# Other step lists for the first and the middle batches of a gated cross-attention and expert kernel, on all engines

## The chip, the cores and the metric

The kernel runs on one core of a Trainium2 chip. The metric is the device time of one execution in microseconds. TensorE is called PE, VectorE DVE, ScalarE ACT, GpSimd POOL and SyncE SP, as the profile does.

## The reference, cut to what matters

x is 8 batches x 512 tokens x 256, the context 8 x 512 x 128. There are 16 heads of 64 and 8 experts of which each token takes 2.

```python
x = x + tanh(g_xattn) * (softmax(q k^T / 8) v @ Wo + bo)   # q = layernorm(x) @ Wq, k, v = ctx @ Wk, ctx @ Wv
h = layernorm(x)
comb = top2(softmax(h @ gate_w.T))                          # 8 weights per token, 6 of them zero
x = x + tanh(g_ffn) * sum_e comb[:, e] * (h @ expert_w[e].T + expert_b[e])
```

## The kernel before

Each fp32 operand is split into two fp16 parts, high and low, and each product is made of three fp16 matmuls (high x high, high x low, low x high).

A batch is worked through in 32 rows, one for each pair of heads p and each tile t of 128 queries (32 = 8 pairs x 4 tiles). The attention of unit n of a batch goes through all engines: PE makes its scores (`scores`, line 1480, six matmuls for the two heads) into one of two PSUM buffers ST, used in turn; DVE takes the negative row maximum (`maximum`, line 1021) and adds a constant (`shift`, line 1027); ACT makes the exponential pf (`exp`, line 832), which frees ST, and copies it to fp16 (`copy`, line 842, p_s high); POOL subtracts to get the low part (`low`, line 654); SP transposes both halves by DMA into pt_s (lines 554 and 561); PE multiplies them with the values (`values`, line 1502, 24 matmuls) and DVE divides (`normalise`, lines 1041 and 1044). pf has 3 slots, p_s 4 and pt_s 8, so that `exp` of unit n waits for `low` of n - 3, `copy` and `low` of n for the transposes of n - 4, and the transpose of n for `values` of n - 8.

Between the scores PE does jobs, each into one of three shared PSUM banks MB in turn: q, k, v (projections, 6, 3 and 3 matmuls), xt and x2t (transposed normalised inputs), ot (transposed outputs of a pair of heads), wo (output projection, 12 matmuls), logits, gates, bias, bound and pair (two tiles through one expert, 12 matmuls). A job of the kind q, k, v, xt, ot or x2t is taken out by ACT (`hi`, high part) and then by DVE (`take`, low part); the others by DVE alone. A job needs the bank of the third job before it, so the `take` of that one.

In what order each engine does all this is written out by hand, one string for each row, in `PE_ORDER`, `ACT_ORDER`, `DVE_ORDER` and `POOL_ORDER`, each with one list for the first batch (`FIRST`), one for the six middle batches (`LOOP`) and one for the last (`LAST`). Every engine walks its own list and waits for semaphores. The n-th `take` or `hi` of a list means the n-th job of PE's list, so a new PE list renumbers them. `values` runs 6 units behind: the first six `values` of a list belong to the batch before (in the first batch they are skipped), and `VALUES_BACK` and its like set that. SP has no list: it walks units in order, `turn_hi` and `turn_lo` of each (lines 554 and 561), with the store of the batch before (line 593) and the load of the next context (line 570) ahead of unit 0, and the load of the next x (line 583) behind unit 9.

In the first batch DVE and ACT also split Wo and the expert weights (`ll`, line 1213, and `lh`, line 817), after maxima (`lm`) and scales (`ls`, with PE's `lsum`). `context` on ACT splits the next context and waits for c_mul, which DVE makes when it takes the job `bound`. `sums1` and `moments1` on DVE (lines 877 and 886) and `power1` and `norm1` on POOL normalise the next x; the same with 2 is for the experts. `route1` to `route3` on DVE choose the experts, and `hold1` to `hold3` make POOL stand still meanwhile.

## Time and profile before

| what | us |
|---|---|
| median of 3 runs (lowest, highest) | 945.15 (944.91, 945.45) |
| the profiled execution, its own time | 948.67 |
| its span, first to last instruction | 946.9 |
| PE, DVE, ACT, POOL busy | 902.7, 852.6, 743.8, 646.3 |

The profiled execution lies 3.5 us above the median, and its span 1.8 us below its own time. The stages are told by the maxima of unit 0 of each batch: the first batch goes from 22.8 to 133.9 us, each middle batch takes 109.7 us (the sixth 111.4 in this execution), and the last goes from 793.7 to the end. A row of a timeline is a time of start, a duration, engine, line and tiles, and in square brackets the idle time of that engine before it and what ended it.

### The profile page before, as it was taken

Reading aid. Unit: us, or ns where it says so; the run is one execution under the profiler, and the core shown is the slowest. Engines: PE = TensorE matmul, PEld = TensorE weight load, DVE = VectorE, ACT = ScalarE, POOL = GpSimd, SP = SyncE. Lnnn points to the kernel's source line nnn. Section 1 sums busy time; section 2 is a strip of 40 time slices with the busy share of each in tenths; the row PEclk is TensorE's granted clock in tenths of the full one; section 3 lists DMA queues with packets and bytes.
Section 4 is the critical chain, followed back from the end, with each engine's and each line's share of the span. In section 5 each row is a group of like instructions: output and inputs, shape, how many; then the busy total and the mean of one; then the engine's idle time right before and its main releaser. Section 6 shows DMA issues by size and latency. Waiting matters only on the chain.

```text
span 946.9 us, 28867 instructions
## 1 busy us (share of the span) xinstructions
PE 902.7 (95%) x11376; PEld 605.1 (64%) x11376; DVE 852.6 (90%) x1853; ACT 743.8 (79%) x1093; POOL 646.3 (68%) x449
## 2 busy tenths in 40 slices
PE   6788799999999999999999999999999999999997
PEld 4245455777657776677657776577655776667873
DVE  6899799998999989999899989999899998999768
ACT  3898899778995879958896879958899588988510
POOL 4677768677695867768586776958687686877400
PEclk9899899999999999999999999999999999999999
DMA  6699899999999999989999999989999799999900
GB/s 222 143 179 167 146 161 190 165 150 165 171 193 149 158 148 197 183 141 157 180 180 160 153 162 189 186 146 157 150 187 187 137 154 171 169 169 164 143 24 23
DMA packets 549142, 150.97 MB, mean 159 GB/s; under 512 B 537592, under 2 KB 547216, under 8 KB 548752
## 3 DMA queue, kind: packets, MB, share of 16 engines
q1 hardware_dynamic: 549008, 149.13, 94.7%
q8 instruction: 91, 1.49, 0.6%
q14 instruction: 43, 0.35, 0.1%
HBM read 11.70 MB, written 4.19 MB: 17 GB/s over the span
## 4 chain that ended last, share of the span: by engine, by line
PE 47%; DVE 25%; ACT 12%; issue 8%; DMA 3%; POOL 3%; SPq 1%; ACTq 0%; DVEq 0%; POOLq 0%
PE MB L1338 24%; PE ST L1480 9%; PE PV L1502 9%; DVE nmax L1021 8%; ACT pf L832 5%; ACT p_s L842 4%; PE MB L1350 3%; DMA pt_s<-p_s 3%; POOL p_s L654 2%; DVE acc L956 2%; DVE QL L1001 2%; DVE x L924 1%; DVE o_n L1044 1%; DVE v_s L1012 1%; ACT v_s L758 1%
## 5 line engine op out<-in xcount | busy, mean ns | idle before, releaser
L654 POOL TENSOR_TENSOR p_s<-pf,p_s 128x1024 f16<-128x1024 f32 x254 | 542.1, 2136 | 217.3 <-ACT p_s L842 169.1
L832 ACT ACTIVATE pf<-ST,shifts 128x512 f32<-128x512 f32 x512 | 324.4, 691 | 92.2 <-DVE shifts L1027 89.9
L1021 DVE TENSOR_REDUCE nmax<-ST 128x2 f32<-128x1024 f32 x256 | 310.4, 1217 | 17.6 <-PE ST L1480 15.8
L842 ACT ACTIVATE p_s<-pf 128x1024 f16<-128x1024 f32 x254 | 270.7, 1069 | 3.2
L1502 PEld LDWEIGHTS PV<-v_s,pt_s 128*128 128x128 f16 x6096 | 204.3, 98 | 43.6 <-issue 27.5
L1502 PE MATMUL PV<-v_s,pt_s 128*128 128x65 f16 x6096 | 215.7, 193 | 4.7 <-DVE o_n L1044 2.7
L1338 PE MATMUL MB<-ex_s,x2t_s 128*128 128x256 f16 (+1 forms) x1380 | 166.8, 276 | 1.1 <-DVE x L924 1.0
L1338 PEld LDWEIGHTS MB<-ex_s,x2t_s 128*128 128x128 f16 x1380 | 131.7, 98 | 23.6 <-DVE x L924 2.3
L1480 PE MATMUL ST<-KH,QH 64*128 64x512 f16 x512 | 100.8, 390 | 16.3 <-ACT pf L832 14.0
L975 DVE SCALAR_TENSOR_TENSOR acc<-MB,m,acc 128x256 f32<-128x256 f32 x224 | 95.6, 476 | 4.4 <-PE MB L1338 3.6
L1480 PE MATMUL ST<-KH,QL 64*128 64x512 f16 x512 | 99.0, 383 | 0.0
L1480 PE MATMUL ST<-KL,QH 64*128 64x512 f16 x512 | 98.8, 382 | 0.0
L1338 PE MATMUL MB<-xt_s,wq_s 128*128 128x512 f16 x384 | 95.0, 384 | 2.8 <-DVE ot_s L1009 1.3
L1338 PE MATMUL MB<-wo_s,ot_s 128*128 128x256 f16 x744 | 91.8, 274 | 0.1
L1338 PEld LDWEIGHTS MB<-wo_s,ot_s 128*128 128x128 f16 x744 | 71.5, 98 | 17.2 <-DVE v_s L1012 2.6
L1480 PEld LDWEIGHTS ST<-KH,QH 64*128 64x128 f16 x512 | 24.9, 93 | 77.8 <-ACT pf L832 34.4
L1338 PEld LDWEIGHTS MB<-xt_s,wq_s 128*128 128x128 f16 x384 | 33.1, 98 | 45.2 <-issue 12.9
L1001 DVE SCALAR_TENSOR_TENSOR QL<-MB,q_out,QH 128x512 f16<-128x512 f32 x64 | 47.5, 743 | 12.4 <-ACT QH L743 12.4
L1044 DVE TENSOR_TENSOR o_n<-PV,rden 128x256 f32<-128x256 f32 x127 | 53.9, 425 | 4.4
L1338 PE MATMUL MB<-wv_s,kv_s 128*128 128x512 f16 x192 | 53.9, 394 | 2.5 <-DVE QL L1001 1.9
L1012 DVE SCALAR_TENSOR_TENSOR v_s<-MB,v_mul,v_s 128x512 f16<-128x512 f32 x64 | 47.0, 748 | 7.8 <-ACT v_s L758 6.4
L1338 PE MATMUL MB<-kv_s,wk_s 128*128 128x512 f16 x192 | 52.3, 382 | 1.4 <-DVE KL L1001 1.3
(174 smaller groups left out, 986.5 us busy)
## 6 DMA issues: line engine op xcount, KB each, us to landing
pt_s<-p_s SPq DMA_TRANSPOSE x508, 3.4
xin<-x SPq DMA_DIRECT2D x7, 512.0 KB, 4.9
out<-acc SPq DMA_DIRECT2D x7, 512.0 KB, 3.9
kvin<-kv_t SPq DMA_DIRECT2D x8, 256.0 KB, 4.4
stage_e<-expert_t SPq DMA_DIRECT2D x1, 2048.0 KB, 11.1
stage_o<-wo SPq DMA_DIRECT2D x1, 1024.0 KB, 5.8
stage_q<-wq SPq DMA_DIRECT2D x1, 768.0 KB, 7.3
xin<-x SPq DMA_DIRECT2D x2, 256.0 KB, 2.9
```

The lines of the kernel that those rows point to most:

```text
L654: pool.tensor_tensor(p_s[:, slot, 1, :, :], pf[:, it.ring(p, u, PF_SLOTS), :, :], p_s[:, slot, 0, :, :], ALU.subtract).then_inc(p_lo, 1)
L832: last = act.activation(pf[:, (n - 1) % PF_SLOTS, i, :], ST[u % 2][:, i, :], ACT.Exp, bias=shifts[:, u % 2, i:i + 1])
L842: act.activation(p_s[:, it.ring(p, u, P_SLOTS), 0, :, :], pf[:, it.ring(p, u, PF_SLOTS), :, :], ACT.Copy).then_inc(p_hi, 1)
L975: last = dve.scalar_tensor_tensor(acc[:, t, :], m[:, DIM * i:DIM * (i + 1)], comb[:, t, e:e + 1], acc[:, t, :], ALU.mult, ALU.add)
L1001: last = dve.scalar_tensor_tensor(l_s[:, slot_, :], m[:, :], scale, h_s[:, slot_, :], ALU.mult, ALU.subtract)
L1012: last = dve.scalar_tensor_tensor(v_s[:, 1, t, g * HH:(g + 1) * HH, 0:HEAD], m[:, :].rearrange("p (h d) -> p h d", d=HEAD), v_mul[:, it.b ...
L1021: dve.tensor_reduce(nmax[:, t % 2, :, 0], ST[t % 2][:, :, :], AX.X, ALU.max, negate=True)\
L1044: dve.tensor_tensor(dst, outs[:, :, 0:HEAD], rden[:, :].unsqueeze(2).broadcast_to([P, TT, HEAD]), ALU.mult).then_inc(o_ready, 1)
L1338: last = pe.matmul(dst, s, m, start=(k == 0), stop=(k == n - 1))
L1350: last = pe.transpose(bank_[:, tile(t)], src(t), ident[:, :])
L1480: last = pe.matmul(ST[t % 2][:, i, :], queries[r, s, tile(t)], keys[r, s, :], start=(n == 0), stop=(n == len(terms) - 1))
L1502: last = pe.matmul(dst, pt_s[:, slot, a, i, k, :], v_s[:, c, k, (2 * p + i) % HEADS, :], start=(k == 0 and n == 0), stop=(k == TT - 1 and ...
```

## The change

The lists of `FIRST` and `LOOP` are replaced for all four engines; those of `LAST` stay, and so does every other line. Each list holds the same steps as often as before (in `LOOP` 129 for PE, 102 for ACT, 153 for DVE, 42 for POOL; in `FIRST` 105, 111, 144 and 37), in another order, and PE's jobs are taken out in that new order. The core of the diff; of DVE's list for the first batch only the new rows are shown. Rows are counted from 0 within a list:

```diff
@@ -68,25 +68,25 @@
 
 PE_ORDER = {
     FIRST: (
-        "scores", "scores pj q2", "scores v0,0 v3,0 values", "scores v1,0 values", "scores",
-        "scores values values v2,0 k2", "scores values q3", "scores q4", "scores values values values",
-        "scores v0,1 values", "scores k3 k4 values", "scores k5", "scores q5", "scores values values lsum ot0 v1,1",
-        "scores", "scores values values v3,1", "scores values values", "scores q6 ot1 values values", "scores v2,1",
-        "scores values k7 values k6", "scores values values", "scores wo0,0 values bound", "scores wo0,1 values ot3",
-        "scores q7 ot2", "scores values values", "scores xt1 values xt0 wo1,1", "scores values", "scores wo1,0 k1",
-        "scores values values q0", "scores values ot4 ot5 values", "scores k0", "scores q1 wo2,0 wo2,1",
+        "scores", "scores pj", "scores v1,0 values values values v3,0", "scores v2,0 v0,0 values",
+        "scores values q2 values", "scores k2 k3 values", "scores values q3", "scores", "scores v0,1", "scores v1,1 k4",
+        "scores values values q4", "scores values values ot0 v2,1", "scores values lsum", "scores v3,1 values", "scores",
+        "scores values values values bound values", "scores k5", "scores values values q5 ot1", "scores q6",
+        "scores wo0,0 values", "scores wo0,1", "scores k6 k7", "scores values q7", "scores ot3 values",
+        "scores ot2 values xt1", "scores values values xt0", "scores values values",
+        "scores wo1,1 values values wo1,0 ot4", "scores", "scores values ot5 q0 k0", "scores values k1",
+        "scores q1 wo2,0 wo2,1",
     ),
     LOOP: (
-        "scores", "scores v3,0 values v2,0 values", "scores", "scores ot6 values values q2 values values",
-        "scores ot7 k2", "scores v0,0 wo3,1", "scores v1,0 wo3,0 v1,1", "scores values q3 values", "scores",
-        "scores q4 values values k3", "scores v3,1 v0,1", "scores k5 values values x2t0 ot0",
-        "scores x2t1 q5 bound values values", "scores ot1 v2,1 logits values values k4", "scores",
-        "scores q6 wo0,0 values values pair0,3 pair0,6 values wo0,1", "scores",
-        "scores values pair1,1 pair1,7 pair0,5 pair0,1 pair1,0", "scores", "scores values ot2 pair1,5 values q7",
-        "scores", "scores values ot3 gates values pair0,0 k6 bias1", "scores", "scores k7 values values pair0,2 wo1,0",
-        "scores", "scores xt0 wo1,1 pair1,4 pair0,4 xt1", "scores",
-        "scores values ot4 values pair1,3 pair0,7 values values", "scores", "scores bias0 q1 k1 values q0 pair1,6 ot5",
-        "scores", "scores values k0 wo2,0 pair1,2 wo2,1",
+        "scores", "scores v1,0 values v2,0 values", "scores v3,0 values values", "scores v0,0 values ot6",
+        "scores k2 values q2", "scores ot7 values values", "scores k3 values", "scores v0,1 wo3,1",
+        "scores wo3,0 values q3", "scores", "scores k4 values ot0 values q4", "scores values bound q5 k5 values",
+        "scores v1,1 x2t1 x2t0", "scores values ot1 values logits v2,1", "scores wo0,1 wo0,0 v3,1 values", "scores",
+        "scores values q6 values k6 pair0,0 pair1,6 values pair0,3", "scores",
+        "scores pair1,4 pair1,7 pair0,1 values pair1,0", "scores", "scores pair1,3 q7 values pair0,6 ot2", "scores",
+        "scores pair1,1 values values pair1,2", "scores", "scores ot3 pair0,7 gates k7 values values pair0,5", "scores",
+        "scores pair0,4 xt0 values wo1,0 bias1 values bias0 xt1", "scores", "scores values wo1,1 values",
+        "scores ot4 q0 ot5 values pair1,5 k0 values", "scores", "scores k1 wo2,1 q1 pair0,2 wo2,0",
     ),
     LAST: (
...
@@ -103,18 +103,18 @@
 
 ACT_ORDER = {
     FIRST: (
-        "exp", "exp ph copy hi hi hi copy", "exp hi copy", "exp copy", "exp hi copy", "exp hi copy", "exp hi copy",
-        "exp hi copy", "exp hi copy", "exp hi copy", "exp hi copy", "exp hi copy", "exp hi copy", "exp lh copy lh",
-        "exp lh copy hi", "exp lh hi copy hi", "exp hi copy", "exp hi lh copy", "exp lh hi copy", "exp hi copy hi",
-        "exp context copy lh", "exp lh hi copy", "exp hi hi copy", "exp lh copy lg", "exp hi copy", "exp hi lh copy",
-        "exp lh copy", "exp lh hi copy hi", "exp hi copy hi", "exp hi copy", "exp hi copy", "exp copy",
+        "exp", "exp ph copy hi hi hi copy", "exp hi copy", "exp hi copy", "exp hi copy", "exp hi copy", "exp hi copy",
+        "exp hi copy", "exp hi copy hi", "exp copy", "exp hi copy hi", "exp hi copy", "exp hi copy lh",
+        "exp lh copy lh lh", "exp lh copy", "exp lh lh hi lh copy", "exp hi copy", "exp hi copy", "exp hi copy lh",
+        "exp lg copy", "exp hi copy hi", "exp hi copy", "exp hi copy", "exp hi copy", "exp hi copy", "exp lh copy hi",
+        "exp context copy lh", "exp hi lh copy", "exp hi hi copy hi", "exp hi copy", "exp hi copy", "exp copy",
     ),
     LOOP: (
-        "exp", "exp copy hi hi hi copy", "exp hi copy", "exp hi copy hi", "exp hi copy", "exp hi copy", "exp copy",
-        "exp copy hi hi", "exp hi copy", "exp hi hi hi copy hi", "exp hi hi hi copy hi", "exp copy", "exp hi copy hi",
-        "exp hi copy logits hi", "exp", "exp copy copy", "exp copy", "exp copy", "exp hi copy", "exp copy hi hi",
-        "exp copy", "exp hi copy hi", "exp copy", "exp copy hi", "exp context copy", "exp copy hi hi", "exp copy",
-        "exp copy", "exp hi copy hi hi", "exp hi copy hi", "exp copy", "exp copy",
+        "hi exp hi copy", "exp hi copy", "exp hi copy hi", "exp hi copy", "exp hi hi copy", "exp hi copy", "exp hi copy",
+        "exp copy", "exp copy hi hi hi", "exp hi copy", "exp hi hi copy", "exp hi hi hi copy hi", "exp hi copy logits",
+        "exp copy", "exp hi copy hi hi", "exp copy", "exp copy", "exp copy", "exp copy", "exp hi copy", "exp hi copy",
+        "exp copy", "exp copy hi", "exp hi copy", "exp copy context hi", "exp copy", "exp copy hi", "exp copy",
+        "exp hi hi hi copy", "exp copy hi hi", "exp hi copy", "exp copy",
     ),
     LAST: (
...
@@ -127,32 +127,31 @@
 
 DVE_ORDER = {
     FIRST: (
...
+        "maximum shift rq", "maximum shift pt", "maximum take shift", "maximum take shift take", "maximum lm shift take",
+        "maximum take shift lm", "maximum normalise take shift lm", "maximum take shift lm",
+        "maximum normalise take shift bound", "maximum normalise normalise shift take",
+        "maximum take take normalise shift lm", "maximum normalise shift lm", "maximum take shift",
+        "maximum ls normalise shift sums1", "maximum",
+        "maximum shift take shift moments1 normalise ll take take take normalise", "maximum",
+        "maximum shift take ll shift ll ll", "maximum take shift take normalise", "maximum ll shift take",
+        "maximum take shift ll", "maximum take shift", "maximum take shift take normalise", "maximum ll shift take",
+        "maximum normalise take shift", "maximum take normalise shift ll take", "maximum normalise shift gp",
+        "maximum take shift take ll normalise take", "maximum take shift ll ll", "maximum take shift",
+        "maximum take take shift take", "maximum ll shift normalise take take take",
     ),
     LOOP: (
-        "maximum shift", "maximum shift normalise", "maximum take shift take normalise",
-        "maximum shift take normalise take", "maximum take shift", "maximum take take shift take",
-        "maximum take shift take", "maximum shift sums2 moments2 normalise", "maximum shift take take",
-        "maximum shift bound take", "maximum take shift normalise take take",
-        "maximum take shift take take normalise take", "maximum shift take normalise take",
-        "maximum shift take take take normalise", "maximum",
-        "maximum shift take take shift take route1 normalise route2 route3 take take", "maximum",
-        "maximum shift shift take take take sums1 take normalise moments1 take", "maximum shift",
-        "maximum take shift take normalise take", "maximum shift take", "maximum take shift take take normalise",
-        "maximum take shift take", "maximum shift normalise take take take", "maximum shift",
-        "maximum take shift take take take", "maximum shift take normalise take", "maximum shift take take normalise",
-        "maximum shift take take", "maximum take shift take take", "maximum take shift",
-        "maximum take take shift normalise take take",
+        "maximum shift", "maximum shift normalise take", "maximum take shift normalise take", "maximum take shift bound",
+        "maximum shift take normalise", "maximum take shift normalise take take", "maximum shift take",
+        "maximum shift take", "maximum take shift take sums2 normalise moments2", "maximum take shift",
+        "maximum normalise take take take shift", "maximum shift take take take",
+        "maximum normalise take take take shift", "maximum shift take take normalise take",
+        "maximum take shift sums1 take", "maximum take normalise route1 take shift",
+        "maximum take route2 shift route3 take take", "maximum take shift normalise take",
+        "maximum shift take moments1 take take", "maximum shift", "maximum take shift take take normalise",
+        "maximum shift", "maximum shift take take normalise take", "maximum take shift take",
+        "maximum shift take take normalise take", "maximum", "maximum take shift shift take take take take normalise",
+        "maximum shift take", "maximum take normalise shift", "maximum take take take shift take normalise",
+        "maximum shift take take take", "maximum take shift take take",
     ),
     LAST: (
...
@@ -171,14 +170,14 @@
 
 POOL_ORDER = {
     FIRST: (
-        "residual low", "low", "low", "low", "low", "low", "low", "low", "low", "low", "low", "low", "low", "low", "low",
-        "low", "power1 low", "low", "low", "low", "low", "norm1 low", "low", "low", "low", "context low", "low",
-        "scale low", "low", "low", "low", "low",
+        "low", "residual low", "low", "low", "low", "low", "low", "low", "low", "low", "low", "low", "low", "low", "low",
+        "power1 low", "norm1 low", "low", "low", "low", "scale low", "low", "low", "low", "low", "low", "low", "low",
+        "context low", "low", "low", "low",
     ),
     LOOP: (
-        "low", "low", "low", "low", "low", "low", "low", "low", "low", "power2 low", "norm2 low", "residual low", "low",
-        "low", "low", "hold1 hold3 hold2 low", "low", "low", "low", "power1 low", "low", "norm1 low", "low", "low", "low",
-        "scale low", "context low", "low", "low", "low", "low", "low",
+        "low", "low", "low", "low", "low", "low", "low", "low", "low", "low", "power2 norm2 low", "residual low", "low",
+        "low", "low", "hold1 low", "hold2 hold3 low", "low", "low", "power1 low", "low", "low", "low", "low", "norm1 low",
+        "low", "low", "low", "scale context low", "low", "low", "low",
     ),
     LAST: (
```

## Rows read from the trace of the kernel before

**Rows 1.** The page: busy us of PE (share of the span), instructions.

```profile
PE 902.7 (95%) x11376; PEld 605.1 (64%) x11376; DVE 852.6 (90%) x1853; ACT 743.8 (79%) x1093; POOL 646.3 (68%) x449
```

**Rows 2.** Windows: length, busy us (instructions) by engine, PE clock, DMA share, GB/s.

```profile
22.80:133.90 111.10, 91.72 (x1035) 48.63 (x1031) 101.21 (x182) 96.23 (x145) 78.54 (x47) 0.91 0.94 161
...
243.55:353.24 109.69, 108.68 (x1420) 74.21 (x1418) 101.47 (x225) 91.36 (x135) 80.60 (x55) 1.00 1.03 166
...
682.31:793.67 111.36, 108.84 (x1420) 74.46 (x1418) 102.08 (x225) 91.36 (x135) 80.58 (x55) 1.00 1.00 165
```

**Rows 3.** Timeline of PE in the second middle batch.

```profile
242.69 0.39 PE L1480 MATMUL ST<-KH,QH 64*128 64x512 f16 x2
...
244.74 0.89 PE L1502 MATMUL PV<-v_s,pt_s 128*128 128x65 f16 x24
245.47 0.81 PE L1338 MATMUL MB<-wv_s,kv_s 128*128 128x512 f16 x3
...
246.93 0.39 PE L1480 MATMUL ST<-KH,QH 64*128 64x512 f16 x2
...
265.31 0.39 PE L1480 MATMUL ST<-KH,QH 64*128 64x512 f16 x2
...
265.96 0.38 PE L1480 MATMUL ST<-KH,QH 64*128 64x512 f16 x2
...
266.71 1.47 PE L1338 MATMUL MB<-xt_s,wq_s 128*128 128x512 f16 x6
268.01 1.62 PE L1502 MATMUL PV<-v_s,pt_s 128*128 128x65 f16 x48
...
281.50 0.39 PE L1480 MATMUL ST<-KH,QH 64*128 64x512 f16 x2 [0.50 <-ACT pf L832]
...
282.25 0.66 PE L1350 MATMUL MB<-ident,o_n 128*128 128x128 f32 x4
282.75 0.81 PE L1338 MATMUL MB<-wv_s,kv_s 128*128 128x512 f16 x3
...
301.66 4.10 PE L1338 MATMUL MB<-ex_s,x2t_s 128*128 128x256 f16 x36 [0.25 <-DVE x L924]
305.69 0.39 PE L1480 MATMUL ST<-KH,QH 64*128 64x512 f16 x2
```

**Rows 4.** Waits in that batch: us in total, times, longest us.

```profile
PEld ST L1480 <- ACT pf L832: 3.1, 8, 0.6
```

**Rows 5.** Timeline of SP in the second and the third middle batch.

```profile
252.28 1.33 SPq L561 DMA_TRANSPOSE pt_s<-p_s  x1
...
258.68 1.34 SPq L561 DMA_TRANSPOSE pt_s<-p_s  x1
...
278.25 1.31 SPq L561 DMA_TRANSPOSE pt_s<-p_s  x1
...
367.54 1.32 SPq L561 DMA_TRANSPOSE pt_s<-p_s  x1
```

**Rows 6.** The tile pt_s: from issue to landing of its transposes, us.

```profile
DMA to landing us min/median/max: 3.0/3.4/6.1
```

**Rows 7.** Waits in the first batch.

```profile
DVE nmax L1021 <- PE ST L1480: 8.0, 6, 3.4
```

**Rows 8.** Timelines of ACT and of DVE in the first batch.

```profile
96.17 0.72 ACT L789 ACTIVATE kv_s<-kvin,c_mul 128x512 f16<-128x512 f32 x1 [3.62 <-DVE c_mul L985]
...
67.89 0.14 DVE L1168 TENSOR_SCALAR eb_mul<-late_mul 128x1 f32<-128x1 f32 x1
...
101.09 1.23 DVE L1021 TENSOR_REDUCE nmax<-ST 128x2 f32<-128x1024 f32 x1 [3.39 <-PE ST L1480]
```

**Rows 9.** Timeline of SP in the first batch, and the tile xin: issue to landing.

```profile
64.61 0.53 SPq L583 DMA_DIRECT2D xin<-x  x1
...
DMA to landing us min/median/max: 2.8/4.5/5.5
```

**Rows 10.** The tile ex_s: ns of one min/median/max, first and last start.

```profile
L1213 DVE SCALAR_TENSOR_TENSOR ex_s<-stage_e,late_mul,ex_s x8: 741/923/1716, 93.0 to 131.1; 128x512 f16<-128x512 f32 x8
```

11 lines of the change are left out of this document (removed).

## The prediction

> **What bounds the kernel now.** The page's busy line comes first: PE is busy 95% of the span, DVE 90% [rows 1]. That is an average over three stages, so I cut the span at the maxima of unit 0 of each batch and read the windows [rows 2]. In a middle batch PE is busy 108.68 of 109.69 us at full clock, DVE 101.47 and ACT 91.36: PE bounds it, six times. In the first batch PE has 91.72 of 111.10, DVE 101.21 and ACT 96.23: DVE bounds it, with 9.9 us of idle. The last batch keeps its lists. So two sums are wanted: PE's waits and its fixed work in the middle, DVE's waits in the first. PE's timeline gives the price of each step [rows 3], the waits who holds it up [rows 4], SP's timeline and the landing of pt_s when the transposes come [rows 5, 6]; for the first batch the same of DVE and ACT [rows 7 to 10].
>
> The profiled execution takes 3.5 us more than the median of the runs. 1.67 of it is the sixth middle batch (111.36 for 109.69), the rest lies outside what changes; the difference is added to the median.
>
> **Middle batches, PE's fixed work.** No step is added or removed; what the order alone changes is how often PE goes from scores to a job and back. Start to start, scores behind scores take 0.65 (265.31 to 265.96), scores before a job 0.75 (265.96 to 266.71), q 1.30 (266.71 to 268.01), values 0.73 (244.74 to 245.47), ot 0.50 (282.25 to 282.75). v and values behind it, up to the scores, take 1.46 (245.47 to 246.93), so v 0.65 and about 0.1 for the way back; three pairs 4.03 (301.66 to 305.69), so 1.31 each and again 0.1 [rows 3]. So a row that holds jobs costs 0.2 more than one of scores alone. Old list: 12 rows are scores alone, 20 hold jobs. New list: 10 and 22. That is +0.4 per batch. With 32 scores, 32 values, 8 q, 16 k and v and the rest at these prices the old list adds up to 107.4 without a wait, the new to 107.8. The other 2.3 of the 109.69 are waits: ACT's exponentials have up to 3.1 in total by the view of waits, 0.6 the longest [rows 4] (part of it overlaps the running matmuls), as the 0.50 at 281.50, where ACT comes out of rows 9 to 12 with eight copies of projections behind it; and takes of DVE, as the 0.25 at 301.66 [rows 3].
>
> **Middle batches, the waits of ACT and DVE.** The new lists put the steps of ACT and of DVE nearer to PE's own order. The eight `hi` that the old list of ACT has in its rows 9 and 10 are ten in rows 8 to 11 in the new one (3, 1, 2, 4), behind copies of units that PE needs no sooner. Walking both engines along PE's new rows at the durations of before I find slack of 0.1 to 0.7 us where the old lists had none. I take 0.5 for all that is left (0 to 2.3: none, or as much as before). DVE's `bound` goes from row 9 to row 3 and there needs the load of the context, behind the store at SP's head; DVE isn't the bound and has 8 us of slack in the batch. Cost 0, up to 1 where PE waits for the take behind it.
>
> **Middle batches, the transposes.** This is what speaks against the change. SP issues them back to back, 1.3 us each (1.33, 1.34, 1.31, 1.32) [rows 5], so two to a unit, 64 to a batch, 85 us; the first ten or so units queue behind one another, since exponentials run ahead of them. The new list takes `values` closer behind: units 0 and 1 in row 5 (7 before), unit 2 in row 6 (9), unit 9 in row 13, units 11 to 13 in row 16 (15, 15, 17). Whether PE then stands is a race that can be counted. Unit 2: ahead of its `values` in the new list stand 7 scores (4.55), 4 v (2.6), 8 values (5.84), 2 k (1.3), 1 q (1.3), 2 ot (1.0) and 5 ways there and back (1.0), together 17.6 us behind the first scores. Its low transpose was issued 16.0 behind them (258.68 - 242.69 [rows 3, 5]) and in the next batch 15.2 (367.54 - 352.38, that is 242.69 and a batch); its landing takes 3.4 in the median [rows 6], so it is there at 19.4 or 18.6; less 0.5, by which the exponentials of the first units come earlier in my walk of the new lists, since the old ones end a batch with ACT behind PE. PE waits 0.5 to 1.3, the mean is 0.9. Unit 9, counted in the same way (14 scores, 15 values, 6 v, 4 k, 4 q, 4 ot, two of wo at the price of a pair, two x2t at that of ot, the small `bound`, 12 rows there and back): 39.5 us of work, the transpose issued at 35.6 (278.25 - 242.69) and landed at 39.0, or at 41.7 with the longest landing of 6.1. PE waits 0 to 2.2; I take 0.5, nearer to what the median landing gives. Units 11 to 13 have a few tenths of margin. What PE loses in the front it doesn't lose again behind, since the transposes catch up. Sum of the transposes: 1.4; the lower bound is nothing (0.5 for unit 2 is within the error of my walk), the upper 1.3 + 2.2 = 3.5.
>
> So a middle batch takes 107.8 + 0.5 + 1.4 = 109.7, as before: +0.0 each, with bounds of -1.4 (0.5 for everything) and +1.6 (3.5 instead of 1.4, less the 0.5 of other waits, which it covers).
>
> The Trainium skill ("DMA: Bandwidth & Descriptors", section "Latency and other measured facts") gives 261 GB/s for DMA transposes; for our 256 KB each that is an estimate of 1.0 us, where the trace has 1.3 [rows 5]. By the page the queue of the first ten units would be 0.3 x 2 us shorter per unit, 1.8 us at unit 2, and the waits above would be gone; that is the rival "to the floor" below, with 108.3 per batch. The trace decides, so I don't take it.
>
> **The first batch.** DVE's idle there is led by 8.0 us of maxima that wait for scores, 3.4 the longest [rows 7]; 1.56 of the 8.0 lies ahead of the window. The longest comes so: `bound` stands in row 21 of PE and row 22 of DVE, `context` in row 20 of ACT. ACT stands 3.62 us for c_mul at 96.17, the exponentials behind it are late, ST isn't free, and DVE stands 3.39 at 101.09 [rows 8]. In the new lists the job stands in row 15 of PE and its take in row 15 of DVE, `context` in row 26 of ACT: it finds c_mul made. -3.4. Its rows move behind the stall, and nobody waits for them but the first projections of the next batch, seven rows on. Of the other 3.1 us of that kind about half goes, since ACT's `lh` and `hi` are spread more evenly and DVE's maxima of rows 14 and 16 stand alone: -1.5 (0 to -3.1). Against it `sums1` moves from row 15 to row 13. It needs the load of x that SP issues at 64.61, landing 4.5 later in the median, at 69.1, at the latest at 70.1 [rows 9]; DVE ends `ls` at 68.0 (67.89 + 0.14 [rows 8]) and would have a division and a shift (0.7, an estimate) to do before `sums1`: it waits 0.4 to 2.1 (from none of it done to the latest landing), more if it keeps a better pace until then. I take 1.5, because I let some of the early waits go. A further 0.2 for `bound` and `moments1` standing nearer to their givers. Sum: -3.4 - 1.5 + 1.5 + 0.2 = -3.2 (-5 to -1).
>
> What the splits `ll` take isn't sure: the eight of ex_s took 741 to 1716 ns, the median 923 [rows 10]. All at the lowest would give back 8 x 0.18 = 1.5 us, and as much could come on top. I take 0, because POOL has a `low` in every row of either list. With that the bounds of the first batch are -5 and 0.
>
> The Trainium skill ("SBUF — State Buffer", section "Who interferes with whom") says that a DVE instruction with two SBUF inputs and a GpSimd instruction that reads SBUF shut one another out for their whole length, which speaks for the long ones [rows 10]. By the page the spread depends on which of the two is issued first; if all eight met a `low` and took the 1716 of the longest, the sum would be 8 x 0.79 = 6.3 us more, and I see nothing in the new order that makes more of them meet.
>
> **Total.** 945.15 - 3.2 + 6 x 0.0 = 942.0 (rounded).
>
> **The rivals.**
> - To the floor. The transposes are early enough, because ACT and POOL start each batch sooner and shorten the whole queue: 107.8 + 0.5 = 108.3, 6 x -1.4, with the first batch 945.15 - 8.4 - 3.2 = 933.6. For it: the store and the load at SP's head don't depend on the lists, and 0.9 us of wait is small beside a landing of 3.0 to 6.1 [rows 6]. Against it: SP is full from unit 0 to unit 9 whatever ACT does [rows 5].
> - The transposes bind (the other side). With the longer landings units 2 and 9 cost 3.5 together, 111.3 a batch: 945.15 + 9.6 - 3.2 = 951.6. It decides from 1.9 us of transpose waits a batch on, where 945.15 is reached. For it: a landing can take 6.1 [rows 6], and the sixth middle batch lost 1.67 in this execution [rows 2]. Against it: the five others lost none.
> - The change doesn't do in the first batch what it seems to: the stall of `context` is only moved. The wait for x at its upper bound, splits beside POOL +1: 0 instead of -3.2, 945.2. For it: DVE has 101.2 of fixed work, and where ACT (96.2) no longer stands, DVE's own order does [rows 2].
>
> **How the numbers follow.** Forecast 0.36, to the floor 0.19, transposes bind 0.23, no gain in the first batch 0.22. A measurement of this kernel tells 0.2%, 1.9 us, from no change: faster is below 943.3, slower above 947.0. The forecast's own range is 939 to 945: 0.26 of its 0.36 is faster, 0.10 same. The floor is faster, the binding case slower. The fourth is 0.05 faster, 0.14 same, 0.03 slower. Faster 0.50, same 0.24, slower 0.26. The range goes from the floor's 933.5 to 951.0, just short of the binding case's bound, and leaves out a tenth at either end.
>
> **What the profile of the changed kernel would show.** Middle batches between the maxima of unit 0: near 109.7; 108.3 would be the floor. Waits of values for pt_s about 1.4 a batch, near rows 6 and 13, where there were almost none; waits of scores for exponentials about 0.5 instead of 3.1. First batch near 107.9, with no wait of `context` for c_mul, one of `sums1` for x of 0.4 to 2.1. The prediction is wrong if the transposes are issued otherwise than back to back, if PE's clock falls below full in a middle batch, or if DVE's queue meets a job's take that I took to be covered.

## The result, and the profile after

The changed kernel takes 954.87 us in the median of six runs (950.31 to 958.13), the kernel before 945.03 in six runs beside it (943.66 to 947.99). The ratio is 1.0101, with a 95% interval of 1.0076 to 1.0125: 1% slower, where 942.0 was forecast, and outside the range of 933.5 to 951.0. The runs spread wider than those of before, over 7.8 us instead of 4.3. The profiled execution is the fastest of the six (950.31, span 948.5), so what it shows is a mild case.

The page after, first row, answers to [rows 1]; busy times have hardly moved, which is right for lists of the same steps.

```profile
PE 899.2 (95%) x11376; PEld 606.0 (64%) x11376; DVE 854.0 (90%) x1853; ACT 751.2 (79%) x1093; POOL 646.0 (68%) x449
```

The windows by batch answer to [rows 2], with the same columns: the first batch and the first four middle ones.

```profile
21.69:129.61 107.92, 88.55 (x1037) 47.84 (x1034) 101.86 (x181) 96.52 (x145) 78.14 (x47) 0.96 0.98 169
129.61:238.27 108.66, 107.78 (x1414) 74.20 (x1413) 101.60 (x226) 91.87 (x134) 80.27 (x54) 1.00 1.02 164
238.27:349.13 110.86, 108.59 (x1420) 74.73 (x1418) 101.69 (x225) 92.72 (x135) 80.70 (x55) 1.00 1.01 165
349.13:463.17 114.04, 110.02 (x1420) 75.13 (x1418) 101.79 (x225) 92.75 (x135) 80.69 (x55) 0.99 1.01 161
463.17:574.07 110.90, 108.80 (x1420) 74.71 (x1418) 101.78 (x224) 92.60 (x135) 80.67 (x55) 1.00 1.03 165
```

The middle batches, of which five took 109.7 before and the sixth 111.4, now take anything from 108.7 to 114.0. (The window of the first holds six matmuls fewer than the others, 1414 instead of 1420, so its 108.66 flatters it.) All six together are 666.0 (129.61 to 795.60) for 659.8 before. The first batch is 107.9, as forecast, in this execution.

What lengthens the third middle batch is seen on PE's timeline, ahead of the values of unit 2 (its first scores start at 348.27), and on SP's, where the low transpose of that unit is the row of 363.59.

```profile
365.95 0.82 PE L1337 MATMUL MB<-kv_s,wk_s 128*128 128x512 f16 x3
368.71 1.34 PE L1501 MATMUL PV<-v_s,pt_s 128*128 128x65 f16 x24 [1.95 <-issue]
369.99 0.61 PE L1479 MATMUL ST<-KH,QH 64*128 64x512 f16 x2
```

```profile
354.36 0.48 SPq L569 DMA_DIRECT2D kvin<-kv_t  x1
354.93 1.89 SPq L553 DMA_TRANSPOSE pt_s<-p_s  x1
356.88 2.54 SPq L560 DMA_TRANSPOSE pt_s<-p_s  x1
359.50 1.26 SPq L553 DMA_TRANSPOSE pt_s<-p_s  x1
360.82 1.33 SPq L560 DMA_TRANSPOSE pt_s<-p_s  x1
362.24 1.30 SPq L553 DMA_TRANSPOSE pt_s<-p_s  x1
363.59 1.33 SPq L560 DMA_TRANSPOSE pt_s<-p_s  x1
```

The transpose is issued 15.3 us behind the first scores and lands 5.0 later, where the median is 3.4 [rows 6]; the values start then, after 1.95 of idle. "issue" says that the profile names no releaser for that row; in sister batches the same row is ended by the DMA of pt_s. SP has no gap. Two transposes of unit 0 took 1.89 and 2.54 instead of 1.3; in the third middle batch of the kernel before the same two took 1.9 and 2.4, so that alone is nothing new. The wait costs more than its length: the values behind it take 1.34 for 0.89 [rows 3], the scores 0.61 for 0.39, for the granted clock is half in that stretch. Two windows show it. It is the only middle batch of this profile where the clock fell; the fourth had a wait of 1.76 ahead of the same values and kept it.

```profile
366.00:369.00 3.00, 1.05 (x14) 0.47 (x13) 2.96 (x6) 2.76 (x5) 2.28 (x2) 0.99 1.24 123
369.00:372.00 3.00, 3.00 (x28) 1.45 (x26) 0.76 (x2) 0.89 (x2) 1.65 (x1) 0.50 0.98 184
```

The same batch has the other place, row 16, ahead of the values of unit 11.

```profile
401.96 0.88 PE L1501 MATMUL PV<-v_s,pt_s 128*128 128x65 f16 x24 [1.36 <-DMA pt_s<-p_s]
```

The kernel before had that wait too, once: the 1.7 us that its sixth middle batch took longer are nearly all a wait for the transpose of unit 11, in its row 15.

```profile
731.42 0.88 PE L1502 MATMUL PV<-v_s,pt_s 128*128 128x65 f16 x24 [1.50 <-DMA pt_s<-p_s]
```

### The profile page after: what moved, and what is told of

Its sections match the earlier page's. It is cut to its first block, busy times and chain, and to the rows that moved or that the text cites. A ratio compares the mean times of both kernels' runs of the same rounds, so it can differ in the third digit from the quotient of the medians.

```text
span 948.5 us, 28867 instructions
## 1 busy us (share of the span) xinstructions
PE 899.2 (95%) x11376; PEld 606.0 (64%) x11376; DVE 854.0 (90%) x1853; ACT 751.2 (79%) x1093; POOL 646.0 (68%) x449
## 4 chain that ended last, share of the span: by engine, by line
PE 58%; DVE 16%; issue 7%; ACT 7%; DMA 6%; POOL 5%; SPq 1%; ACTq 0%; DVEq 0%; POOLq 0%
PE MB L1337 29%; PE ST L1479 12%; PE PV L1501 11%; POOL p_s L653 4%; DVE nmax L1020 4%; ACT pf L831 4%; DMA pt_s<-p_s 3%; PE MB L1349 3%; ACT p_s L841 3%; DMA kvin<-kv_t 1%; PE ST L1337 1%; DVE QL L1000 1%; DVE acc L955 1%; DVE o_n L1043 1%; DVE ot_s L1008 1%
## 5 line engine op out<-in xcount | busy, mean ns | idle before, releaser
L1501 PEld LDWEIGHTS PV<-v_s,pt_s 128*128 128x128 f16 x6096 | 210.2, 98 | 58.7 <-issue 36.5
L1501 PE MATMUL PV<-v_s,pt_s 128*128 128x65 f16 x6096 | 222.2, 194 | 14.8 <-DMA pt_s<-p_s 7.4
L1337 PE MATMUL MB<-ex_s,x2t_s 128*128 128x256 f16 (+1 forms) x1380 | 170.3, 276 | 0.2
L1337 PEld LDWEIGHTS MB<-ex_s,x2t_s 128*128 128x128 f16 x1380 | 129.7, 98 | 32.6 <-DVE acc L974 7.3
L1479 PEld LDWEIGHTS ST<-KH,QH 64*128 64x128 f16 x512 | 25.4, 93 | 68.0 <-issue 27.1
L742 ACT ACTIVATE QH<-MB,q_out 128x512 f16<-128x512 f32 x64 | 44.8, 700 | 21.2 <-PE MB L1337 20.7
L746 ACT ACTIVATE KH<-MB,k_mul 128x512 f16<-128x512 f32 x64 | 45.2, 706 | 17.1 <-PE MB L1337 16.9
L1337 PEld LDWEIGHTS MB<-xt_s,wq_s 128*128 128x128 f16 x384 | 35.1, 99 | 34.4 <-issue 2.9
L757 ACT ACTIVATE v_s<-MB,v_mul 128x512 f16<-128x512 f32 x64 | 45.0, 708 | 11.2 <-PE MB L1337 11.2
```

Source lines behind the costliest of these rows:

```text
L742: last = act.activation(QH[:, it.pair_slot(name), :], m[:, :], ACT.Copy, scale=q_out[:, of % 2:of % 2 + 1])
L746: last = act.activation(KH[:, it.pair_slot(name), :], m[:, :], ACT.Copy, scale=k_mul[:, of % 2:of % 2 + 1])
L757: last = act.activation(v_s[:, 0, t, g * HH:(g + 1) * HH, 0:HEAD], m[:, :].rearrange("p (h d) -> p h d", d=HEAD), ACT.Copy, scale=v_mul[:, ...
L1337: last = pe.matmul(dst, s, m, start=(k == 0), stop=(k == n - 1))
L1479: last = pe.matmul(ST[t % 2][:, i, :], queries[r, s, tile(t)], keys[r, s, :], start=(n == 0), stop=(n == len(terms) - 1))
L1501: last = pe.matmul(dst, pt_s[:, slot, a, i, k, :], v_s[:, c, k, (2 * p + i) % HEADS, :], start=(k == 0 and n == 0), stop=(k == TT - 1 and ...
```

## The experiments

A number such as 945.5 beside them is the median of the kernel before in the same set of runs, on the same chip. Where experiments of different sets are set against one another, the sets' own medians of the kernel before lie between 945.2 and 945.8.

**New lists for the first batch only.**

```diff
 FIRST: new on all four engines
 LOOP:  old on all four engines
```

> New lists for the first batch on all engines, the old ones for the middle batches. In the changed kernel's profile unit 0 of the second batch starts 4.3 us earlier than before (129.6 against 133.9). Theory (the first batch gains, the middle batches lose by late transposes): 945.0 - 4.3 = 940.7, middle batches 109.7 each as before. Rival (the first batch's gain is of that one execution, or is given back at the seam of the lists): 945.

Measured: 950.79 (944.11 to 952.43, 10 runs) for 945.48, ratio 1.0045 (1.0026 to 1.0064). Both guesses fell: the kernel does not gain 4.3, it loses 5.3. Four of its six middle batches are 109.7 to 109.8 as before, the two others 110.8 and 111.3; the first batch is 115.13 in this profile. One of the ten executions took 944.11, so the list can also run as fast as the old one.

```profile
21.26:136.39 115.13, 92.86 (x1037) 50.40 (x1034) 104.50 (x182) 96.90 (x145) 78.49 (x47) 0.90 0.89 159
```

The same list took 107.92 in the changed kernel's profile, so two executions of one list can be laid side by side. They part in rows 13 to 20. First DVE in this experiment:

```profile
68.27 1.41 DVE L878 BATCH_NORM_STATS2 stats<-xin 128x6 f32<-128x256 f32 x4 [2.04 <-DMA xin<-x]
...
82.00 2.38 DVE L1214 SCALAR_TENSOR_TENSOR wo_s<-stage_o,late_mul,wo_s 128x512 f16<-128x512 f32 x1
84.31 0.14 DVE L1028 TENSOR_REDUCE shifts<-nmax 128x2 f32<-128x4 f32 x1
84.38 3.27 DVE L1214 SCALAR_TENSOR_TENSOR wo_s<-stage_o,late_mul,wo_s 128x512 f16<-128x512 f32 x2
```

and the same in the changed kernel:

```profile
67.62 1.41 DVE L876 BATCH_NORM_STATS2 stats<-xin 128x6 f32<-128x256 f32 x4 [0.95 <-DMA xin<-x]
...
79.51 1.95 DVE L1212 SCALAR_TENSOR_TENSOR wo_s<-stage_o,late_mul,wo_s 128x512 f16<-128x512 f32 x1
81.39 0.14 DVE L1026 TENSOR_REDUCE shifts<-nmax 128x2 f32<-128x4 f32 x1
81.45 1.40 DVE L1212 SCALAR_TENSOR_TENSOR wo_s<-stage_o,late_mul,wo_s 128x512 f16<-128x512 f32 x2
```

Then PE in this experiment:

```profile
73.62 1.48 PE L1503 MATMUL PV<-v_s,pt_s 128*128 128x65 f16 x24 [2.75 <-DVE o_n L1045]
...
90.16 2.74 PE L1339 MATMUL MB<-wo_s,ot_s 128*128 128x256 f16 x12 [3.49 <-DVE ot_s L1010]
```

and in the changed kernel:

```profile
72.98 0.88 PE L1501 MATMUL PV<-v_s,pt_s 128*128 128x65 f16 x24 [1.20 <-DVE o_n L1043]
...
85.36 1.49 PE L1337 MATMUL MB<-wo_s,ot_s 128*128 128x256 f16 x12 [0.62 <-DVE ot_s L1008]
```

DVE waits a us more for x, and the division comes 0.65 later (73.05 for 72.40). PE is 0.9 ahead here and stands 2.75 for it instead of 1.20. The clock had fallen to half ahead of that wait in both (68.7 here, 68.5 there, behind 2.0 us of idle for the exponentials); there it is full again from 72.0, here only from 79.0, and the 24 matmuls take 1.48 for 0.88. In row 17 the three splits beside POOL start 2.5 later and take 5.65 for 3.35, the take of ot1 is 4.8 late, PE stands 3.49 instead of 0.62, and the clock is at half again until 96.0. Between the two executions lie 7.2 us.

DVE's own work has grown as well. Its busy time in the first batch is 104.5 here, 104.3 to 104.6 in four more profiles of the new list and 101.9 in the changed kernel's, but 99.1 to 102.2 in seven profiles of the old one. The splits are a part of it (15.7 us for the twelve here, 14.3 in the profile before). The other part is one instruction of the step `gp`, moved from row 30 to row 26, which the prediction doesn't mention: the split of the expert bias, 0.47 us in every profile of the old list and 2.40 to 2.43 in all six of the new. The tile view before and here:

```profile
L1175 DVE SCALAR_TENSOR_TENSOR eb_s<-eb,eb_mul,eb_s x1: 474/474/474, 128.6 to 128.6; 8x256 fp32r<-8x256 f32 x1
L1176 DVE SCALAR_TENSOR_TENSOR eb_s<-eb,eb_mul,eb_s x1: 2414/2414/2414, 115.3 to 115.3; 8x256 fp32r<-8x256 f32 x1
```

**New lists for the middle batches only.**

```diff
 FIRST: old on all four engines
 LOOP:  new on all four engines
```

> Old lists for the first batch, new ones for the middle batches. Theory: the loss is all in the middle, 954.9 + 4.3 = 959.2, some 2.3 us for each of the six batches. Rival (the loss needs both, since the new first list hands the middle batches a worse start): 945 to 950.

Measured: 952.25 (950.84 to 957.54, 5 runs), ratio 1.0087 (1.0060 to 1.0113). The middle lists lose 6.8 us by themselves, 1.1 a batch. With the 5.3 of the first lists that is 12.1 for the 9.8 measured together: within the spread of the runs, the two losses add up. The theory had put all of it in the middle and was half right.

**Six values moved back.**

```diff
 PE:  -"scores ot7 values values", "scores k3 values", "scores v0,1 wo3,1"
      +"scores ot7", "scores k3 values values", "scores v0,1 wo3,1 values"
      -"scores values q6 values k6 pair0,0 pair1,6 values pair0,3"
      +"scores q6 k6 values pair0,0 values pair1,6 pair0,3 values"
 DVE: division of units 0, 1 from row 5 to row 6, of 10, 11 from row 15 to row 16
```

> The changed kernel, with only the values of units 0 to 2 (one row later, behind the jobs of their row) and of units 11 to 13 (behind q6 and k6 in the same row) moved back in the middle list of PE, and the two divisions behind them on DVE. Theory (PE stands only for transposes that have not landed, since SP issues them back to back): those waits go, a middle batch takes about 108.1, 954.9 - 6 x 3.9 = 931.5; at least below 940. Rival (the new order of the takes and the exponentials is what makes PE wait, late transposes only stand in its place): 950 to 957, with waits of scores and jobs for ACT and DVE in their place.

Measured: 960.99 (958.74 to 966.74, 4 runs), ratio 1.0175 (1.0140 to 1.0210). A miss, and its own fault. Units 0 to 2 no longer wait in its profile, but the values of unit 12 need the division of units 10 and 11, which the edit had put behind the take of k6, and PE stands there for 1.75 to 1.90 us in each of the six middle batches. In three of them it comes back slow (here 14 matmuls of the pairs in 2.69 us, where the 12 ahead of the wait took 1.47):

```profile
297.52 1.47 PE L1380 MATMUL MB<-ex_s,x2t_s 128*128 128x256 f16 x12
300.89 0.89 PE L1544 MATMUL PV<-v_s,pt_s 128*128 128x65 f16 x24 [1.90 <-DVE o_n L1086]
301.62 2.69 PE L1380 MATMUL MB<-ex_s,x2t_s 128*128 128x256 f16 x14
```

That gives the price of a fall of the clock, since the wait is nearly the same everywhere: with the fall a batch takes 112.2, 112.7 and 113.1, without it 111.0 to 111.3, so some 1.5 us more. The third and the sixth batch, both with 1.90 us of wait there:

```profile
359.71:472.76 113.05, 110.12 (x1420) 75.72 (x1418) 101.79 (x225) 92.58 (x135) 80.66 (x55) 0.98 0.99 162
694.83:806.12 111.29, 108.44 (x1420) 74.86 (x1418) 101.84 (x225) 92.61 (x135) 80.69 (x55) 1.00 1.00 165
```

So the length of that wait alone doesn't tell which it will be. The front and row 16 were parted, below.

**SP's store and load later.**

```diff
 SP, middle batches:
-store, load of the next context, unit 0, unit 1, unit 2, ...
+unit 0, unit 1, unit 2, store, load of the next context, unit 3, ...
 DVE: bound from row 3 to row 9
```

> The changed kernel, with the store and the load of the next context behind the transposes of unit 2 instead of ahead of those of unit 0 in SP's order of the middle batches, and bound in row 9 of DVE instead of row 3, since its load comes later. Theory: the transposes of units 0 to 2 are issued about 1.2 us sooner (0.58 + 0.48 and the gaps), the wait for unit 2 shrinks by that, those for units 11 to 13 stay: 954.9 - 6 x 1.1 = 948. Rival (not SP's queue but the copies and low parts set when the transposes go, or the takes of DVE set PE's waits): no change, 955.

Measured: 952.21 (948.00 to 953.49, 5 runs), ratio 1.0066 (1.0044 to 1.0087), 2.7 below the changed kernel (the two intervals overlap, so the gain in time is likely, not certain). In its second middle batch (first scores at 244.51) the low transpose of unit 2 is issued 14.0 behind them, and its values follow k3 without a wait; nowhere in the fronts of its six middle batches is there one of 0.3 us or more:

```profile
258.55 1.33 SPq L580 DMA_TRANSPOSE pt_s<-p_s  x1
259.93 0.58 SPq L616 DMA_DIRECT2D out<-acc  x1
260.62 0.48 SPq L589 DMA_DIRECT2D kvin<-kv_t  x1
```

```profile
261.53 0.82 PE L1361 MATMUL MB<-kv_s,wk_s 128*128 128x512 f16 x3
262.19 0.90 PE L1525 MATMUL PV<-v_s,pt_s 128*128 128x65 f16 x24
```

No list of PE, ACT or POOL differs from the changed kernel's, and on DVE only `bound` stands elsewhere, so it is SP's queue that the front waits for. (That `bound` had a share wasn't tested by itself, but the waits that went had been for the transposes.) Of the expected 6.6 us only 2.7 came. The waits in row 16 stay, as expected; new ones, for the transposes of units 5 and 6, stand in rows 10 and 11 in four of the six batches, 0.92 to 1.66 us:

```profile
385.86 0.88 PE L1525 MATMUL PV<-v_s,pt_s 128*128 128x65 f16 x24 [1.66 <-DMA pt_s<-p_s]
```

**Front values later**, with the old first list.

```diff
 PE:  -"scores ot7 values values", "scores k3 values", "scores v0,1 wo3,1"
      +"scores ot7", "scores k3 values values", "scores v0,1 wo3,1 values"
 DVE: -"maximum take shift normalise take take", "maximum shift take"
      +"maximum take shift take take", "maximum shift take normalise"
```

> Old first list, new middle lists, and in these only the values of units 0 to 2 one row later (with the division of units 0 and 1). Baseline is the kernel with the old first and the new middle lists, 952.3. Theory (in the front PE stands for transposes that are late by 0.8 to 2.2 us a batch, and most of it is given back once it stands less, some of it is taken again at row 16, where PE now comes earlier): 946, between 943 and 949. Rival (as the kernel with six values moved back, which took 961: moving values costs PE more than it saves): 952 or more.

Measured: 946.17 (943.25 to 948.49, 10 runs) for 945.34, ratio 1.0014 (1.0003 to 1.0025). The theory's number: 6.1 us of the 6.8 come back by three `values` moved by one row, with the division of two units.

**Front and row 16 later.**

```diff
 as above, and
 PE:  -"scores values q6 values k6 pair0,0 pair1,6 values pair0,3"
      +"scores q6 values k6 pair0,0 values pair1,6 pair0,3 values"
 DVE: -"maximum take normalise route1 take shift"
      +"maximum take route1 take shift normalise"
```

> As the one before, and in row 16 the values of unit 11 behind q6 and those of unit 12 behind pair0,0, with the division of units 10 and 11 at the end of DVE's row 15 instead of its middle. Theory: nothing stands for transposes any more, a middle batch takes 108.3 to 108.8, 940 (937 to 943). Rival (values of unit 12 need the division of units 10 and 11, so that PE stands for DVE instead, as it did for 1.9 us in the kernel with six values moved back): 946 to 950.

Measured: 942.14 (941.59 to 944.11, 8 runs), ratio 0.9972 (0.9962 to 0.9983): faster than before, and with 2.5 us the narrowest spread of the experiments. Two of its middle batches:

```profile
240.93:350.25 109.32, 108.54 (x1420) 74.69 (x1418) 101.61 (x224) 92.45 (x135) 80.64 (x55) 1.00 1.02 168
350.25:460.25 110.00, 108.55 (x1420) 74.66 (x1418) 101.62 (x224) 92.24 (x135) 80.64 (x55) 1.00 1.06 167
```

The theory's 108.3 to 108.8 is not there. Three of the six batches still wait 0.56 to 0.90 us for a transpose in row 11 or 13. The six together take 658.4 in this profile, the slowest of the eight executions, and 659.8 in the profile before: 1.4 of the 3.2 us gained are seen there, the rest isn't located.

**sums1 later in the first batch**, with the new first and the old middle lists.

```diff
 DVE FIRST: sums1 from row 13 to the end of row 15, moments1 to row 16
 POOL FIRST: power1, norm1 one row later each
```

> New first list, old middle lists, and in the first batch only sums1 moved back from row 13 to the end of row 15 on DVE, moments1 to row 16, power1 and norm1 on POOL one row later each. Baseline is the kernel with the new first and the old middle lists, 950.8. Theory (DVE stands 1 to 2 us for x, the division behind it is late, PE stands 2.75 us for it and its clock falls to half until row 16): the wait and the first fall of the clock go, 948 (946.5 to 949). Rival (the first batch loses by the splits of row 17 alone): 950 to 951.

Measured: 946.63 (944.96 to 948.64, 10 runs) for 945.34, ratio 1.0017 (1.0006 to 1.0028). 4.2 us come back, 2.8 were expected. The wait for x is gone and PE stands 1.14 for the division in row 15 instead of 2.75, and 1.29 for a transpose behind it; at wo0,0 it still stands for the take, and runs at half clock behind it:

```profile
71.86 0.88 PE L1553 MATMUL PV<-v_s,pt_s 128*128 128x65 f16 x24 [1.14 <-DVE o_n L1095]
...
87.40 2.71 PE L1389 MATMUL MB<-wo_s,ot_s 128*128 128x256 f16 x12 [2.15 <-DVE ot_s L1060]
```

**sums1 later and the splits spread.**

```diff
 DVE FIRST, beside the above: of row 17's three ll one goes to row 14, one to row 16
```

> As the one before, and the three splits of row 17 on DVE are one each in rows 14, 16 and 17. Theory (three splits in a row beside POOL's low parts put the take of ot1 back by 2 us, PE stands 3.5 us for it at wo0,0 and its clock falls again until row 20): the second fall goes as well, 943 (941 to 945), below before. Rival (a split takes as long wherever it stands, and DVE, which bounds the first batch, ends no sooner): as the kernel without the spread, 948.

Measured: 947.10 (945.10 to 948.31, 10 runs), ratio 1.0017 (1.0006 to 1.0027). Nothing gained; the rival is right. The second stall did go:

```profile
87.43 1.48 PE L1389 MATMUL MB<-wo_s,ot_s 128*128 128x256 f16 x12 [0.39 <-DVE ot_s L1060]
```

But the first batch takes 111.4 us in this profile and 111.3 in that of the experiment above. Waits for exponentials (1.22, 0.99 and 1.17 us) stand in its place, and DVE is busy 104.6 us here and 104.5 there, with 15.8 us of splits in both.

**Short low parts on POOL.**

```diff
 POOL, first batch, units 12 to 31:
-p_s low, all 512 columns
+p_s low, columns 0 to 15
```

The low part of the other 496 columns is left out, so this kernel is a probe and no candidate.

> New first list, old middle lists; in the first batch POOL makes the low part of units 12 to 31 for 16 of 512 columns only, so that the rest of their low parts is left out and POOL is nearly idle beside the splits of Wo and the expert weights. Baseline is the kernel with the new first and the old middle lists, 950.8; the wait for x stays. Theory (the splits pay for POOL's low parts, 15.7 us for twelve where the shortest would give 8.7, and the late take behind them costs a fall of the clock): all splits take 0.70 to 0.75 us, 943 (940 to 945). Rival (the splits' length varies for another reason, or is covered): 949 to 951.

Measured: 941.04 (938.61 to 943.23, 10 runs) for 945.79, ratio 0.9951 (0.9936 to 0.9967), 9.7 below the same lists with whole low parts. All twelve splits now take 0.74 us; the tile views of this run and, last, of the run with the new first lists:

```profile
L1215 DVE SCALAR_TENSOR_TENSOR wo_s<-stage_o,late_mul,wo_s x4: 739/742/743, 71.9 to 81.1; 128x512 f16<-128x512 f32 x4
L1215 DVE SCALAR_TENSOR_TENSOR ex_s<-stage_e,late_mul,ex_s x8: 739/742/747, 86.3 to 121.5; 128x512 f16<-128x512 f32 x8
```

```profile
L1214 DVE SCALAR_TENSOR_TENSOR wo_s<-stage_o,late_mul,wo_s x4: 735/1561/2609, 73.4 to 85.0; 128x512 f16<-128x512 f32 x4
```

So it is POOL's low parts that lengthen them. The Trainium skill ("SBUF — State Buffer", section "Who interferes with whom") says that a DVE instruction with two SBUF inputs contends with a GpSimd instruction that reads SBUF. This run agrees: 0.74 us here, for up to 2.6 beside whole low parts. The split of the expert bias is back to 0.47 too:

```profile
L1177 DVE SCALAR_TENSOR_TENSOR eb_s<-eb,eb_mul,eb_s x1: 474/474/474, 107.1 to 107.1; 8x256 fp32r<-8x256 f32 x1
```

8.9 us of splits instead of 15.7 and 0.5 instead of 2.4 for the bias are 8.7 of the 9.7. That is arithmetic, not a test of its own: low parts that come earlier and the clock may have a share.

**One step of the new list in the kernel before.**

```diff
 DVE FIRST, old list:
-"maximum take shift normalise ls" ... "maximum normalise sums1 shift"
+"maximum take shift normalise ls sums1" ... "maximum normalise shift"
```

> The kernel before with one step moved: sums1 of the first batch from row 15 to the end of row 13 on DVE, as in the new list. Theory: DVE stands 1 to 2 us for x, which it didn't before, and PE's stall behind it may cost some clock: 946.5 to 948, against 945.4. Rival (the wait is covered, since DVE stood for scores in the same rows anyway): 945.4.

Measured: 948.40 (946.80 to 950.99, 10 runs) for 945.79, ratio 1.0029 (1.0013 to 1.0045). The 2.6 us are more than DVE's wait for x in its profile (1.0). Of the rest two things are seen: q6 runs at half clock there, 2.38 us for 1.46, and two middle batches, whose lists are the old ones, take 110.8 and 110.5, with waits of 0.80 and 0.76 ahead of values. How the rest divides stays open.

```profile
77.97 2.38 PE L1359 MATMUL MB<-xt_s,wq_s 128*128 128x512 f16 x6 [1.26 <-DVE ot_s L1030]
```

**SP's order and row 16**, with the old first list and the front values where the new list has them.

```diff
 SP: store and load behind unit 2; DVE: bound in row 9
 PE and DVE: row 16 later, as above
```

> Old first list, new middle lists; SP's store and load behind the transposes of unit 2 (bound in row 9 of DVE), and in row 16 the values of units 11 and 12 later as in the kernel that took 942.1; the values of units 0 to 2 stay where the new list has them. Theory (either way of freeing the front does, and this one leaves SP ahead by a us until row 13 too): 941 (939 to 943). Rival (the store and the load only meet the transposes later, at units 9 to 12): 944 to 946.

Measured: 946.29 (944.26 to 948.58, 10 runs) for 945.79, ratio 1.0006 (0.9989 to 1.0023). No gain, as the rival said, but the waits aren't at units 9 to 12, where it put them. PE stands 0.77 to 2.55 us in row 11 in four of the batches (and 1.06 in the front of the first):

```profile
605.22 0.88 PE L1547 MATMUL PV<-v_s,pt_s 128*128 128x65 f16 x24 [2.55 <-issue]
```

The transpose of unit 6, for which it stands here, was issued at 598.98 and landed 6.2 us later. Two causes are mixed: PE, hardly held up in the front, comes to this row earlier, and that transpose is issued later, 27.1 us behind the first maximum in the mean of the six batches for 26.4 in the changed kernel. The runs don't part them.

**Rows 11 and 13 later as well.**

```diff
 as front and row 16, and PE:
-"scores values bound q5 k5 values" ... "scores values ot1 values logits v2,1"
+"scores bound q5 values k5 values" ... "scores values ot1 logits values v2,1"
```

> As the kernel that took 942.1 (old first list, new middle lists, values of units 0 to 2, 11 and 12 later), and the first values of row 11 behind bound and q5, the second of row 13 behind logits. In its profile PE stood 1.0 us in row 11 of one middle batch and 0.8 in row 13 of another. Theory (the remaining late transposes are these): a middle batch takes 109.3, 940 (938.5 to 941.5). Rival (what is left is PE's own work and the takes, or they move to the next values): 942.

Measured: 943.30 (942.01 to 945.24, 12 runs) for 945.16, ratio 0.9978 (0.9967 to 0.9988). No further gain, and nothing of the expected 109.3: its middle batches take 109.6 to 110.3, one of them with 1.28 us of wait for a transpose in row 11. The rival, though 1.2 above its number.

Not tried: matmuls without use that keep PE busy in the first batch's stalls, which would have parted the clock's share from the waits' there, and `gp` moved back to row 30 by itself.

## Why the prediction was wrong, point by point

The forecast was +0.0 for a middle batch and -3.2 for the first. Measured alone, the new middle lists cost 6.8 us and the new first lists 5.3. Three terms of the sum failed in the middle and two in the first batch.

**The transposes of the middle batches: right mechanism, too small, and the third place dismissed.** The rival "the transposes bind" is what happened, and was given 0.23. The first step that failed is "Sum of the transposes: 1.4": the six batches of the changed kernel's profile wait 11.0 us for them (waits of 0.3 and more), 1.8 a batch, and those of the run with the new middle lists alone 11.9, 2.0 a batch. For unit 2 the mean was nearly right: 0.35 to 1.95, 1.1 for 0.9. But its waits follow its own landings and not the median of all: 3.4 us, and waits of 0.35 and 0.44, in two batches, 4.5 to 5.0 and waits of 0.53 to 1.95 in the four others. The trace before had it: unit 2 landed after 3.3 to 3.4 in three batches and 4.3 to 4.7 in three. Unit 9, priced at 0.5, never waited. Units 11 to 13, passed over with "a few tenths of margin", stood 1.3 to 1.4 us in three of the six batches; unit 11's low transpose takes 4.0 to 4.8 us to land in all six batches of the trace before, and of the 1.67 of its sixth batch, which the prediction quotes, 1.50 was that wait. Unit 1, not counted, stood up to 0.45.

**The clock, put at nothing.** The price of a wait was taken as its length. Behind the longest one the clock was at half, as in the batch of 114.04, whose PE is busy 110.0 us for 108.6 and 108.8 in its neighbours: 1.3 us, or 0.2 for the mean of the six. The prediction had named a clock below full as a sign of being wrong, but given it no term.

**"SP issues them back to back, 1.3 us each".** Back to back, yes; each 1.3, no. That is the median; the mean is 1.4 and one in seven takes over 1.7 (70 of 508 in the kernel before, up to 2.9 us; 71 in the changed one, up to 3.2), so a batch has 90 us of them and not 85. That the kernel before has as many means that they are not what is new. Nor do they explain why the changed kernel's runs spread over 7.8 us: the new first lists with the old middle ones spread over 8.3.

**"What PE loses in the front it doesn't lose again behind".** It holds for the changed kernel's unit 9. Its reverse I had not thought of: freed in the front through SP, PE stood in rows 10 and 11. How much of that is PE coming earlier, and how much the transposes there being issued later, isn't shown.

**PE's fixed work and the other waits.** 107.8 + 0.5 = 108.3 was to be the floor, and this is the largest error of the middle sum. Batches without late transposes take 109.1 to 109.3 (109.32 above), so fixed work and other waits are 109.2, not 108.3: the new order gives back some 0.4 us of a batch, not 1.4. The reading that failed stands in [rows 2]: of 109.69 us PE was busy 108.68, so there was 1.0 of idle to win. The prediction had 107.4 of fixed work by prices from start to start and called the other 2.3 waits, with the 3.1 of [rows 4] as their source; those are waits of PE's weight loads, and most of them overlap running matmuls. They did shrink, to 1.6 to 2.2 a batch in the changed kernel, and PE's busy time stayed at 108.6 to 108.8 (110.0 with the fall of the clock). The rival "to the floor" at 933.6 has no run near it; the best variant that computes everything is at 942.1.

**The first batch: "Sum: -3.4 - 1.5 + 1.5 + 0.2".** The stall for c_mul is gone, as said, and DVE waits 0.95 to 2.04 us for x, as said. The first step that failed is what stands behind that wait: I priced it as DVE's own 1.5 and did not ask, as one should of any wait added, who is queued behind it: the division, for which PE stood 2.75, with the clock at half until 79.0. Moving sums1 back alone returned 4.2 us. The second is "I take 0" for the splits, and leaving the step `gp` out of them: the twelve take 13.6 to 15.8 us in the six profiles of the new list with whole low parts and 13.4 to 15.4 in the seven of the old, 1.0 more in the mean, and the bias 1.9 more each time, on the engine that bounds the batch. Even with sums1 back, the new first list (946.6) isn't better than the old. And DVE's idle time, out of which 3.4 + 1.5 were to come, was 9.9 us in the profile before but 7.3 to 8.5 in the five others of the same list; with the new list and sums1 back it was 6.8. Where the rest of the c_mul stall's 3.4 went stays open.

**The sum of the profiled execution.** The old first list took 109.4, 107.6, 109.9, 109.1 and 110.0 in five later profiles, so its 111.1 [rows 2] was a slow one. A gain of 3.2 against it was partly a gain against chance, and so are the 107.9 of the changed kernel's profile, which look like the forecast: with the new first lists alone the median was 5.3 above before.

## What to carry to other kernels

Where a queue is full, a step that needs its result has a margin, and the margin is worth as much as the list: read issue and landing of that unit's transfer in every batch of the trace, take the latest and not the median, and place the consumer behind that. A wait of PE that nears 2 us can cost some 1.5 us more in clock, so the price of a new wait includes what PE does behind it. What an order can win on the engine that bounds is about its idle time in the windows, not the sum of the waits in the list. On the engine that bounds, look for every step whose length hangs on its neighbour, the small ones too. And when two lists are exchanged at once, test each alone: here two losses of 5 and 7 us hid a middle list with which the kernel is 0.3% faster once six `values` are placed later.

## What the runs showed of the hardware

PE's granted clock stood at half, 1.2 instead of 2.4 GHz, behind idle times of 1.95 (0.50 in the window from 369 to 372), 2.15 and 3.49 us. The length of the idle time alone didn't decide: behind 1.90 us it fell in one middle batch and not in another of the same run; behind 2.0 us for the exponentials in the first batch it fell in the changed kernel and not with sums1 later; behind 1.20 us the values ran at full clock, but q6 behind 1.26 us ran at half with sums1 moved in the old list. One fall cost a middle batch some 1.5 us.

A DVE split with two operands in SBUF takes 0.74 us with POOL nearly idle and up to 2.6 beside POOL's low parts; the small split of the bias 0.47 and 2.4. SP's transposes of 256 KB take 1.3 us each to issue in the median, 1.4 in the mean, and up to 3.8 (in the run with the store and the load later); from issue to landing they take 3.4 in the median and up to 6.1 in the kernel before [rows 6].
